# A new order of the opening: tokens loaded first, the scale as row products of 288 moving columns, and low parts of the first weights on POOL too

## The reference

```python
mod = jax.nn.silu(c) @ ada_w.T + ada_b
shift_msa, scale_msa, gate_msa, shift_mlp, scale_mlp, gate_mlp = jnp.split(mod, 6, axis=-1)
h = modulate(rmsnorm(x, g1, D), scale_msa, shift_msa)   # x / |x| * sqrt(D) * g1 * (1 + scale) + shift
qkv = h @ qkv_w.T + qkv_b
# q, k normalised per head, softmax attention, projection, gated residual
# then a second rmsnorm and modulate, fc1, gelu, fc2, gated residual
```

## Time and profile before

| | |
|---|---|
| median of 3 runs | 2885.67 us (2885.53 to 2886.21) |
| the profiled execution, its own time | 2886.55 us |
| its span in the profile | 2884.8 us, 35304 instructions |
| busy, share of the span | PE 99%, PEld 75%, DVE 68%, ACT 55%, POOL 7% |
| granted clock of TensorE, mean | 1.00 (0.998) |
| first QKV matmul, end of the first tile's waits | 31.3 us, 43.2 us |

### The profile page before, as it was taken

The page is one execution under the profiler, slowest core; times in us unless marked ns, Lnnn a source line. Parts: engine busy times, 40 slices in busy tenths (PEclk is TensorE's granted clock), DMA queues, the critical chain, the costliest instruction groups (busy, mean ns, idle before and its releaser), DMA issues.

```text
span 2884.8 us, 35304 instructions
## 1 busy us (share of the span) xinstructions
PE 2858.4 (99%) x12990; PEld 2172.0 (75%) x12990; DVE 1971.2 (68%) x2727; ACT 1574.2 (55%) x1924; POOL 215.5 (7%) x163
## 2 busy tenths in 40 slices
PE   8999999999999999999999999999999999999999
PEld 7999995666666666666666666788888888888887
DVE  7777677899898889888989987844344243424342
ACT  4334326777677677677677676634344343434342
POOL 1322310101000000000000000090000000000000
PEclk9999999999999999999999999999999999999999
DMA  6455554322222222222222223432222222322121
GB/s 231 158 190 177 181 162 141 89 74 64 82 81 78 79 83 64 78 84 79 75 79 71 75 84 94 132 127 87 75 87 74 82 79 87 98 91 87 41 69 50
DMA packets 238454, 282.67 MB, mean 98 GB/s; under 512 B 34960, under 2 KB 144016, under 8 KB 237392
## 3 DMA queue, kind: packets, MB, share of 16 engines
q1 hardware_dynamic: 233408, 270.80, 30.5%
q10 hardware_dynamic: 4880, 9.70, 1.0%
HBM read 195.50 MB, written 84.67 MB: 97 GB/s over the span
## 4 chain that ended last, share of the span: by engine, by line
PE 94%; DVE 3%; ACT 1%; DMA 1%; issue 1%; SPq 0%; POOL 0%; POOLq 0%; DVEq 0%; ACTq 0%
PE ps L1651 16%; PE ps L1676 16%; PE ps L1721 15%; PE ps L1739 15%; PE ps L1663 14%; PE ps L798 12%; PE ps L1697 4%; PE ps L1662 2%; PE ps L753 1%; ACT gated L1320 1%; DMA gain<-kg 0%; DVE p_lo L1463 0%; DVE x L1523 0%; PE ps L745 0%; DVE w_lo L1516 0%
## 5 line engine op out<-in xcount | busy, mean ns | idle before, releaser
L1264 ACT ACTIVATE p_r<-ps 128x1024 f32<-128x1024 f32 x512 | 494.2, 1067 | 397.5 <-PE ps L1651 397.5
L1463 DVE TENSOR_TENSOR p_lo<-p_r,p_hi 128x1024 fp32r<-128x1024 f32 x512 | 613.5, 1219 | 0.0
L1651 PE MATMUL ps<-qT,kT 128*128 128x512 f32 x2048 | 570.2, 395 | 3.4 <-DMA kT<-qk_hi_scratch 2.3
L1264 ACT ACTIVATE prob<-ps 128x1024 f32<-128x1024 f32 x512 | 484.0, 1056 | 3.6 <-PE ps L1651 3.6
L1651 PEld LDWEIGHTS ps<-qT,kT 128*128 128x128 f32 x2048 | 381.0, 189 | 133.9 <-issue 51.4
L1662 PE MATMUL ps<-prob,vp 128*64 128x512 f32 x1024 | 453.1, 595 | 0.0
L1663 PE MATMUL ps<-prob,vp 128*37 128x512 f32 x1024 | 451.7, 594 | 0.0
L1593 DVE TENSOR_TENSOR a_lo<-act,a_hi 128x512 fp32r<-128x512 f32 x144 | 101.4, 704 | 502.1 <-ACT a_hi L1307 502.1
L1457 DVE CAST p_hi<-p_r 128x1024 fp32r<-128x1024 f32 x512 | 350.2, 694 | 128.5 <-ACT p_r L1264 124.2
L1739 PE MATMUL ps<-a_hi,w 128*128 128x512 f32 x1296 | 410.8, 389 | 0.0
L1676 PE MATMUL ps<-p_hi,vx 128*128 128x512 f32 x1024 | 399.3, 390 | 0.6 <-issue 0.2
(11 more groups left out here) (195 smaller groups left out, 3561.9 us busy)
## 6 DMA issues: line engine op xcount, KB each, us to landing
w_raw<-w SPq DMA_DIRECT2D x144, 320.0 KB, 2.9
qk_hi_scratch<-aw SPq DMA_DIRECT2D x32, 576.0 KB, 3.2
qk_lo_scratch<-aw SPq DMA_DIRECT2D x32, 576.0 KB, 4.4
kT<-qk_hi_scratch SPq DMA_DIRECT2D x128, 144.0 KB
qT<-qk_hi_scratch SPq DMA_DIRECT2D x128, 144.0 KB
v_scratch<-stv SPq DMA_DIRECT2D x32, 512.0 KB, 2.6
vp<-v_scratch SPq DMA_DIRECT2D x16, 1024.0 KB, 8.9
xb<-xT SPq DMA_DIRECT2D x8, 1280.0 KB, 10.8
```

The source lines that it names most:

```text
L1264: act.activation(out, ps[:, 2 * slot:2 * slot + 2, :].rearrange("p a b -> p (a b)"), ACT.Exp).then_inc(exp_done, 1)
L1463: dve.tensor_tensor(p_lo[:, j], p_r[:, j], f32(p_hi[:, q % HIGHS]), ALU.subtract).then_inc(plo_done, 1)
L1651: mm = pe.matmul(ps[:, 2 * (entry % RING) + h, :], kT[r][:, h, kt * P:(kt + 1) * P], qT[:, u % 2, h], start=True, stop=True)
```

## The change

- **DMA order and kind.** The tokens come right behind c and the small constants; the weights of the scale and of the shift follow. The four gain broadcasts are gone: gains and bias of mod arrive as one tensor `small` of 34 columns. The QKV bias is issued right behind the four weight pieces. The other batch's tokens wait for `mod_mm`, the next modulation weights for `rows_mm`.
- **Scale.** `modulate(ks)`: the two columns of c are now stationary, the weights of `ada` (channels by rows, 576 columns, not 640) are the moving side, in two halves of 288 columns that go to PSUM partitions 0 and 64, so that each chunk has a pair of matmuls. Chunks 0 and 1 stand before the sum of squares, 2 to 4 behind it. ACT copies the two rows out (`rows_out`), and five small matmuls stand them upright again (`upright`) behind `spread_norm`.
- **Spreading of c.** `spread_c(b)` for each batch on its own; PE waits for ACT's copy of batch 0 before it starts batch 1, since they use each other's banks for the last chunk.
- **Sum of squares.** DVE's `sum_first` takes each square as it comes.
- **Shift.** DVE does the norm first and then the five dots of batch 0. The five of batch 1 go to the first tile (three) and to the second (two, between the evacuation of half 0 and `bounded`). The two dots of the next modulation that stood in tile 1 move to tile 2.
- **Weights.** ACT splits pieces 0 and 1 in halves and in a new order, and piece 2 behind all five `high_first`. The low parts of chunks 2 to 4 of pieces 0 and 1 are made by POOL. On DVE, `scaled` and `h0_low` of chunks 2 to 4 now follow each other chunk by chunk.
- Two semaphores are merged into one (`pads`), with the waits adapted.

The diff, cut to its core:

```diff
-    awp = aw[:, 1].rearrange("p (k c) -> p k c", k=KC)
     aws, awn = (aw[:, j, 0:KC * D].rearrange("p (m c) -> p m c", m=KC) for j in range(2))
+    by_rows = awn
+    mrow = xb[0:B, 1].rearrange("p k n -> p (k n)")[:, 0:DP]
+    early_prod = tmp[:, 2:4].rearrange("p k n -> p (k n)")[:, 0:D]
...
-    RB, MOD1 = ps[:, 4, :], ps[:, 5, 0:KC * B].rearrange("p (m b) -> p m b", b=B)
+    RB = ps[:, 4, :]
+    MODT = ps[:, 5, 0:KC * B].rearrange("p (m b) -> p m b", b=B)
     RT = RB[:, 0:2 * TPB].rearrange("p (t c) -> p t c", c=2)
-    CT = RB[:, 0:P].rearrange("p (b c) -> p b c", b=B)
+    CT = [ps[:, 7 - b, 0:TL] for b in range(B)]
...
         sp.dma_start(c_t[:], cT).then_inc(c_ld, 16)
-        sp.dma_start(adab_t[:], adab).then_inc(small_ld, 16)
-        sp.dma_start(awp, ada).then_inc(aw_ld[1], 16)
-        sp.dma_start(aws, adan[0]).then_inc(aw_ld[0], 16)
+        sp.dma_start(small_t[:], small).then_inc(small_ld, 16)
         sp.dma_start(xb[:, 0], xT[:, :, 0:BLK]).then_inc(x_ld[0], 16)
-        for j in range(4):
-            sp.dma_start(gain[:, j:j + 1], gains[j].partition_broadcast(P)).then_inc(gain_ld, 16)
+        sp.dma_start(by_rows, ada).then_inc(aw_ld[0], 16)
+        sp.dma_start(aws, adan[0]).then_inc(aw_ld[1], 16)
         load_w(0)
         load_w(1)
         load_w(2)
         load_w(3)
+        sp.dma_start(bias[:], qkvb.partition_broadcast(P)).then_inc(bias_ld, 16)
         sp.wait_ge(zero_done, 1)
         sp.dma_start(m_s.rearrange("m (a n) -> m a n", a=B * N // BLK),
                      f32(h_lo[0:2 * H, 1, 0]).unsqueeze(1).to_broadcast([2 * H, B * N // BLK, BLK])).then_inc(zero_dma, 16)
+        sp.wait_ge(mod_mm, 1)
         sp.dma_start(xb[:, 1], xT[:, :, N:N + BLK]).then_inc(x_ld[1], 16)
-        sp.wait_ge(dot_done, KC + 2)
-        sp.dma_start(bias[:], qkvb.partition_broadcast(P)).then_inc(bias_ld, 16)
-        sp.wait_ge(mod_mm, 1)
+        sp.wait_ge(rows_mm, 1)
...
+        for q in range(2):
+            pool.wait_ge(whi_done, 2 * q + 2)
+            ks, cols = W_HALVES[1], slice(q * PIECE, (q + 1) * PIECE)
+            pool.tensor_tensor(w_lo[:, ks, cols], raw[q][:, ks], f32(w_hi[:, ks, cols]), ALU.subtract).then_inc(wlo_pool, 1)
         pool.wait_ge(zero_dma, 16)
...
+        def split_half(q, half):
+            if half == 0:
+                act.wait_ge(w_ld[q], 16)
+            ks = W_HALVES[half]
+            act.activation(w_hi[:, ks, q * PIECE:(q + 1) * PIECE], raw[q][:, ks], ACT.Copy).then_inc(whi_done, 1)
...
+        def spread_c(b):
+            act.wait_ge(cb_mm, b + 1)
             act.activation(c_b[:, b, 0:KF * P], ps[:, 6 + b, :], ACT.Copy).then_inc(cb_done, 1)
-        act.activation(c_b[:, :, KF * P:D], CT, ACT.Copy).then_inc(cb_done, 1)
+            act.activation(c_b[:, b, KF * P:D], CT[b], ACT.Copy).then_inc(cb_done, 1)
+        def rows_out():
+            act.wait_ge(rows_mm, 1)
+            low, high = ps[0:B, 0, 0:D // 2], ps[64:64 + B, 1, 0:D // 2]
+            act.activation(mrow[:, 0:D // 2], low, ACT.Copy).then_inc(rows_done, 1)
+            act.activation(mrow[:, D // 2:D], high, ACT.Copy).then_inc(rows_done, 1)
+            act.activation(mrow[:, D:DP], high[:, D // 2 - TL:D // 2], ACT.Copy).then_inc(rows_done, 1)
+        def high_first(m):
+            act.wait_ge(aff_done, m + 1)
+            act.activation(h_hi[:, 0, m], tmp[:, m], ACT.Identity,
...
+        spread_c(0)
         act.wait_ge(x_ld[0], 16)
         for m in range(KC):
             act.activation(tmp[:, m], xb[:, 0, m], ACT.Square).then_inc(sq0_done, 1)
-        split_w(0)
+        spread_c(1)
         norm_act(act, 0)
-        split_w(1)
-        for m in range(KC):
-            act.wait_ge(aff_done, m + 1)
-            act.activation(h_hi[:, 0, m], tmp[:, m], ACT.Identity,
-                           bias=mod[:, SHIFT_MSA, m, 0:1], scale=1.0).then_inc(hhi0_done, 1)
-            if m == 1:
-                split_w(2)
+        rows_out()
+        split_half(0, 0)
+        split_half(0, 1)
+        split_half(1, 0)
+        high_first(0)
+        high_first(1)
+        split_half(1, 1)
+        for m in range(2, KC):
+            high_first(m)
+        split_w(2)
         split_w(3)
-        act.wait_ge(wlo_done, 2)
+        act.wait_ge(wlo_done, 1)
+        act.wait_ge(wlo_pool, 1)
...
+        def sum_first():
+            for k in (1, 2):
+                dve.wait_ge(sq0_done, k + 1)
+                dve.tensor_tensor(tmp[:, 0], tmp[:, 0], tmp[:, k], ALU.add).then_inc(sqsum, 1)
+                dve.wait_ge(sqsum, k)
+            dve.wait_ge(sq0_done, KF)
+            dve.tensor_tensor(tmp[:, 0], tmp[:, 0], tmp[:, KF - 1], ALU.add).then_inc(sqsum, 1)
+            dve.wait_ge(sqsum, KF - 1)
+            dve.wait_ge(sq0_done, KC)
+            dve.tensor_tensor(tmp[0:TL, 0], tmp[0:TL, 0], tmp[0:TL, KF], ALU.add).then_inc(sqsum, 1)
+            dve.wait_ge(sqsum, KF)
+            dve.tensor_copy(sq_hi[:], tmp[:, 0]).then_inc(sqhi_done, 1)
+            dve.wait_ge(sqhi_done, 1)
+            dve.tensor_tensor(sq_lo[:], tmp[:, 0], f32(sq_hi[:]), ALU.subtract).then_inc(sqlo_done, 1)
...
-            dve.wait_ge(whi_done, q + 1)
+            dve.wait_ge(whi_done, 2 * q + 1 if q < 2 else q + 3)
...
-        dve.wait_ge(cb_done, 3)
-        dve.wait_ge(aw_ld[0], 16)
-        for m in range(KC):
-            shift(0, m, bias[:, 0:D])
-        for m in range(2):
-            shift(1, m, bias[:, 0:D])
-        dve.wait_ge(gain_ld, 64)
...
-        dve.wait_ge(sq0_done, KC)
-        sum_chunks(dve, 0)
-        dve.tensor_scalar(root_gain[:], gain[:, 0:1], float(D) ** 0.5, None, ALU.mult).then_inc(gain_b, 1)
+        sum_first()
+        bounded(dve, 0)
+        reciprocal(dve, 0)
+        dve.wait_ge(cb_done, 2)
+        dve.wait_ge(aw_ld[1], 16)
+        for m in range(KC):
+            shift(0, m, early_prod)
+        w_low(0, 0, wlo_done)
         dve.wait_ge(mod_mm, 1)
         dve.wait_ge(adab_one, 1)
-        dve.tensor_tensor(mod[:, SCALE_MSA], MOD1, adab_t[:, KC:2 * KC].unsqueeze(2).to_broadcast([P, KC, B]),
+        dve.tensor_tensor(mod[:, SCALE_MSA], MODT, adab_t[:, KC:2 * KC].unsqueeze(2).to_broadcast([P, KC, B]),
...
-        dve.wait_ge(gain_b, 1)
         dve.wait_ge(mod_done, 1)
         dve.tensor_scalar(mod[:, SCALE_MSA], mod[:, SCALE_MSA], root_gain[:, 0:1], None, ALU.mult).then_inc(mod_done, 1)
-        w_low(0, 0, wlo_done)
-        bounded(dve, 0)
-        reciprocal(dve, 0)
-        w_low(0, 1, wlo_done)
         dve.wait_ge(mod_done, 2)
         dve.wait_ge(modn_add, 1)
         dve.wait_ge(rb_mm, 1)
         scaled(0)
+        scaled(1)
         w_low(1, 0, wlo_done)
         h0_low(0)
-        scaled(1)
-        w_low(1, 1, wlo_done)
-        scaled(2)
         h0_low(1)
-        scaled(3)
-        h0_low(2)
-        scaled(4)
-        h0_low(3)
-        h0_low(4)
+        for m in range(2, KC):
+            scaled(m)
+            h0_low(m)
         dve.wait_ge(aff_done, KC)
         dve.tensor_copy(warm[:], gain[:, 0:1]).then_inc(xr_done, 1)
         for half in range(2):
             for q in (2, 3):
                 w_low(q, half, wlo_last)
         dve.wait_ge(bias_ld, 16)
-        dve.wait_ge(wlo_done, 4)
+        dve.wait_ge(wlo_done, 2)
+        dve.wait_ge(wlo_pool, 2)
...
-        DOTS_FIRST = ((), (0, 1), (), (2, 3, 4))
+        DOTS_FIRST = ((), (), (0, 1), (2, 3, 4))
...
+                    if first and r == 0 and t == 1:
+                        for m in range(3, KC):
+                            shift(1, m, prod)
...
                     if first and r == 0 and t == 0:
-                        for m in range(2, KC):
+                        dve.wait_ge(cb_done, 2 * B)
+                        for m in range(3):
                             shift(1, m, prod)
...
-        def modulate(m):
+        def modulate(ks):
+            for k in ks:
+                rows = slice(0, P if k < KF else TL)
+                for half in range(2):
+                    mm = pe.matmul(ps[64 * half:64 * half + B, half, 0:D // 2], c_s[rows, k],
+                                   by_rows[rows, k, half * D // 2:(half + 1) * D // 2], start=k == 0, stop=k == KC - 1)
+            return mm
+        def upright():
+            pe.wait_ge(rows_done, 3)
+            for m in range(KC):
+                mm = pe.matmul(MODT[:, m], mrow[:, m * P:(m + 1) * P], ident[0:B, 0:B], start=True, stop=True)
+            mm.then_inc(mod_mm, 1)
...
+        def spread_c(b):
+            wait(pe, cb_done, 2 * b)
...
+        spread_c(0)
+        spread_c(1)
+        pe.wait_ge(aw_ld[0], 16)
+        modulate(range(2))
         pe.wait_ge(ones_done, 2)
         sum_squares(0)
+        modulate(range(2, KC)).then_inc(rows_mm, 1)
         spread_norm(0)
+        upright()
...
-                            pe.wait_ge((wlo_done, wlo_last)[h], 3 - h)
+                            pe.wait_ge((wlo_done, wlo_last)[h], 2)
                         if k == W_HALVES[1].start:
```

(29 more changed lines are left out.)

63 lines of the change are left out of this document (31 added, 32 removed).

## The result

The changed kernel takes 2890.29 us (median of 20 runs, 2889.16 to 2891.86), the kernel before 2885.97 (20 runs beside them, 2885.37 to 2887.99): a ratio of 1.0015, 95% interval 1.0009 to 1.0021, or 4.3 us more. It is within 0.2%, but above the range that was predicted (2882.6 to 2888.6). The profiled execution has a span of 2888.4, 3.6 above the old one, and a mean granted clock of 0.998 like before. So the places where 3.6 us came in can be looked for in it. (The medians differ by 0.7 more, since the old profiled execution, 2886.55, was one of the longer ones of its kernel.)

A forecast was written before the change was run, and what follows sets the result against it. PE, busy 99% of the span, bounds the kernel, through the opening's last low part at 43.2. +0.2 there and +0.3 in the second tile make +0.5 on 2886.55; the median, 0.88 below, is 2886.2, range 2882.6 to 2888.6.

The forecast's parts named there:

- the two holds: Opening: POOL's low parts hold DVE's scale TENSOR_SCALAR and `h0_low(2)`, each up to 1.6 us, counted in full.
- the landing: Opening transfers: tokens land at about 7.8 us, scale rows at 11.3, shift rows at 14.8, piece 0 at 17.5.
- three low parts taken at their free price: End of the opening: DVE's three low parts behind piece 3 take 1.0 + 1.4 + 1.5 us, ending at 43.4.
- two moved dots taken at nothing: Tile 2: the two dots moved from tile 1 fall into DVE's idle time, with no cost added.
- the clock's rival: First tile: PE waits before half 1 and resumes at the lower clock, +1.5 to +4.1 us, 2887.7 to 2890.3; chance 0.13.
- Spreading, pairs, sums, `spread_norm`, `upright`: Opening on PE: spreading to 10.6 us, pairs 0.96 each, sums 1.9, `spread_norm` 2.09 to 20.2, `upright` to 22.5.
- The rival that the pairs don't run side by side: Scale matmuls in the opening: five pairs cost 4.8 us more, giving 2891.0; chance 0.05.
- the largest of the rivals: Opening: POOL doesn't hold `h0_low(2)`, 2884.6 us, nor the scale either, 2883.0; chance 0.36, both together.
- The order of ACT's splits: Opening: ACT splits piece 2 only behind chunk 4's high part, to 37.6 us, and piece 3 to 39.5.
- Tile 1's stall of 0.3: Second tile: two dots before `bounded` and the reciprocal take 1.7 us, so PE waits 0.3.
- the slack of 1.35: Second tile: the reciprocal ended at 57.04 and PE wanted it at 58.39; 1.35 us doesn't hold the two dots.
- Changes below 0.2% (5.8 us) can't be told from none: Whole kernel: the measurement's resolution is 0.2%, 5.8 us; chance 0.94 that the result lies within it.

The follow-up runs named there:

- e14: Changed kernel with SP waiting for the first tokens' landing before issuing the scale's weights: span 2891.7 us, 3.3 more than the changed kernel's.
- e2: Changed kernel with ACT's split of piece 2 moved from behind high_first(4) to behind high_first(2): 2888.61 us, ratio 1.0008.
- e4: Changed kernel with the two dots of the next modulation moved back from tile 2 to tile 1: 2890.2 us, ratio 1.0013.
- e7: Changed kernel with gain and adab_t as two SBUF tensors in their old places, filled by two DMAs: span 2887.0 us.
- e8: Changed kernel with input tensor small padded from 34 to 350 columns, only 34 loaded: span 2889.7 us, end-of-QKV stretch 38.62 us.
- e1: Changed kernel with the low parts of chunks 2 to 4 of pieces 0 and 1 made by DVE again, not POOL: 2888.35 us, ratio 1.0008.
- e6: Kernel before with an unused SBUF tensor of 30 columns, moving large buffers 128 bytes: span 2884.7 us, end-of-QKV stretch 38.79 us.
- e9: Changed kernel with the edits of e1, e2, e4 and e7 in one: 2884.59 us, ratio 0.9993.
- e13: Kernel before with an unused SBUF tensor of 48 columns, moving large buffers 192 bytes: span 2887.1 us, end-of-QKV stretch 38.78 us.
- e3: Changed kernel with POOL's sums of squares of the second block held until the last w_low is done: span 2888.5 us.

## Why the prediction was wrong, point by point

The forecast was +0.5 us for the profiled execution; it came out at +3.6. The mechanism was right up to the scale and in the two holds; the terms that failed are the landing, three low parts taken at their free price, two moved dots taken at nothing, and the place of the buffers, which had no term. The time of 2890.3 is the upper end of the clock's rival only by chance: that rival cost 0.1.

- **Landings, mis-sized by 1.5 us.** The step that failed first is "Tokens in the first place land at 8.35 less the 0.33 MB". They came at 9.34, the weights of the scale at 12.8 in place of 11.3. The step worked with bytes alone: it took over the 6.7 us of another transfer and shortened them (by the 0.4 MB/us that it names, 0.33 MB less would even be 7.5, not 7.8). The tokens took 7.70 with others behind them and 6.57 alone (e14).
- **Spreading, pairs, sums, `spread_norm`, `upright`:** right. Two pairs took 2.1 (predicted 2.0), three 3.1, `spread_norm` 2.1, `upright` 2.3. The rival that the pairs don't run side by side falls. Scale in at 24.05, 1.5 late by the landing alone.
- **The port, two holds:** right in place and size (1.4 and 1.2 lost; predicted 1.6 each), against the largest of the rivals. The Trainium skill's rule ("SBUF — State Buffer", "Who interferes with whom") agrees with these rows and with the next ones. I had applied it only to instructions that the change added.
- **The third hold, 1.1 us, not foreseen.** "Of DVE's four last low parts three stand behind piece 3: 1.0 + 1.4 + 1.5" took 4.98. POOL's sums of the next block begin when ACT has squared it (42.59), and ACT squares right behind its last split, as DVE starts the three; so both move together, and being late isn't the reason. In the kernel before they met in the same way, and POOL waited:

```profile
41.67 4.04 POOL L319 TENSOR_TENSOR tmp<-tmp 128x512 f32<-128x512 f32 x2 [37.88 <-ACT tmp L377]
```

There the last low part starts at 41.68, 0.01 behind the add's record. In all six traces with the hold (the changed kernel, e2, e4, e7, e8, e14) it starts 0.05 to 0.06 behind it, in the nine without (both profiles of the kernel before, e1, e6, e9 to e13) 0.01 to 0.02. All six have POOL make low parts and none of the nine has; what shifts POOL by these hundredths stays open. e3 removes the hold, and alone gives nothing back.
- **The order of ACT's splits:** right. Its last one ended at 40.37 for 39.5, late by what was left of the landing: later starts had made the two holds 0.2 and 0.4 shorter than predicted. e2 puts its price at 1.8.
- **The clock.** It fell, as the rival said, with a chance of 0.13 only. Against it the prediction set that "no gap of the old trace lost the upper level", and it read the granted clock as 1.00 throughout. Both are misreadings. At the end of the QKV stage the old trace has a PE gap of 2.98 us (to 435.60), its granted clock in 435 to 443 is 0.50, and the ten matmuls of 512 columns at 443.88 take 0.43 each (4.32 in all), where the later ones take 0.23. So a fall behind some 3 us was more likely than that. It cost the changed kernel only 0.1 (PE's first twelve matmuls ended at 45.5, the low part at 45.38). It stood right behind: each repair of DVE's side alone (e1, e3) lost about 1.1 to it.
- **Tile 1's stall of 0.3:** absent. PE came 2.2 later and the reciprocal 2.9 (59.73 against 56.84), so the dots took 0.7 of the slack of 1.35 and not 1.7. The first dot of tile 0, which had taken 1.55 beside POOL's last sum, took 0.75: that sum ended at 52.00, before the dot (52.52).
- **"In tile 2 the two moved dots fall into DVE's idle time": wrong, 0.75 us.** The time was idle on DVE and not on POOL, whose low part of 4.6 us stood in it. The first dot took 2.61. It is the rule used above, not applied to a moved instruction.
- **The place of the buffers, 1.4 us, not foreseen.** The change's list called the constants one tensor of 34 columns and the prediction counted it as a DMA alone. That it moves kT and all behind it by 128 bytes, off a multiple of 256, was not looked at.
- **"Changes below 0.2% (5.8 us) can't be told from none":** too coarse. 20 runs each tell the 4.3 us from none (1.0009 to 1.0021).

The sum of what was measured: 2.2 in the opening (of it about 0.9 landing, 1.1 the third hold, 0.2 as predicted), 0.75 in tile 2, 1.4 at the end of the stage, less 0.4 given back by then and 0.4 later, make the 3.6 of the spans. These are shares along the chain and not what each repair gives back: the third hold gave nothing alone, since the clock stood behind it, and no run gives the landing back. What stays open is how the 256 bytes act, why the tokens' transfer is slow for its bytes, and why the landing of one kernel's tokens differs by 1 us from one execution to the next.

## What to carry to other kernels

When work is moved to a second engine that shares a port, check every long two-input instruction of the first engine against every instruction of the second in the new order, not only those that moved. Where two such instructions start within a few hundredths of a us of each other, count the hold as possible, though the trace before doesn't show it. When PE's own gap grows, price the last low part and PE's own backlog at the lower clock as two limits side by side, since repairing one alone shows nothing. And when a small tensor is added ahead of large ones in SBUF, look at where the large ones then begin.

## What the runs showed of the hardware

- A DVE instruction with two SBUF inputs, or a short TENSOR_SCALAR, waits for the end of a POOL subtraction: 0.23 became 1.60, 0.74 became 1.93, a dot of 0.75 became 2.61. DVE instructions that follow each other without a pause can keep POOL out in turn: two of its adds took 4.01 and not 2.65. A POOL add that was ready 0.05 to 0.06 us ahead of the next DVE subtraction went first in six traces, one that was ready 0.01 to 0.02 ahead waited in nine.
- PE's rise to the upper level in one and the same program came at 37.7 and at 40.6 (0.9 us at the next tile's sums). Behind a gap of 3.0 us PE fell to the lower level (granted clock 0.50 to 0.63) in all seven traces (the changed kernel, e1, e3, e4, e7, e8, e14) and stayed there for some 2.9 to 6.2 us; behind one of 1.15 it fell in e2 and not in e9; with the gap filled by 14 matmuls it didn't.
- Transfers were slower with the large buffers 64, 128 or 192 bytes off a multiple of 256: two stores of 576 KB out of SBUF landed after 3.5 and 5.1 us in place of 3.1 and 4.4; at the end of the QKV stage the first kT issue took 1.5 to 1.6 us in place of 1.1, and the stretch 38.6 to 39.2 in place of 36.7 to 37.8.
